# One Trainium2 kernel of a conv-attention hybrid: when the pair operands are asked for, one transfer for both copies' rows, and a table built through a skewed view

## The reference

```python
def layer0(x):                                  # 6 heads of 16 channels, 1024 tokens
    q, k, v = split(groupnorm(x) @ qkv_w + qkv_b)
    attn = (q * SCALE) @ k.T + rel_h[:, :, :, None] + rel_w[:, :, None, :]
    return x + softmax(attn) @ v @ proj_w + proj_b      # rel_w = q . rel_pos_w[w - w' + 31]
def layer1(t):
    att = where(causal, (q @ k.T) * scale, -big)        # of layernorm(t)
    return t + softmax(att) @ v @ w_proj
t = layer1(layer0(x)); out = t + experts(layernorm(t))  # top 2 of 4
```

## Time and profile before

| what | value |
|---|---|
| median of 3 runs | 2129.08 us |
| the profiled execution's own time | 2129.47 us |
| its span, first to last instruction | 2127.6 us |
| TensorE busy | 1741.9 us (82%) |
| VectorE, ScalarE, GpSimd busy | 1222.2, 1073.3, 294.8 us |
| share of the chain that ended last: PE, DVE, DMA | 53%, 20%, 12% |
| in it, waits for the transfer `qr<-negb` | 4% |
| in it, waits for `qs<-scr_rel`, for `qs<-negr` | 4%, 2% |
| mean granted TensorE clock | 0.915 of full speed |

### The profile page before, as it was taken

How to read it: one execution, slowest core, us unless ns; L and a number is a source line. 1 busy time by engine, 2 the same in 40 slices (tenths; PEclk the granted TensorE clock), 3 DMA queues, 4 the chain that set the end, 5 groups by cost and what they waited for, 6 DMA issues and landing times.

```text
span 2127.6 us, 25037 instructions
## 1 busy us (share of the span) xinstructions
PE 1741.9 (82%) x8928; PEld 694.9 (33%) x8928; DVE 1222.2 (57%) x2526; ACT 1073.3 (50%) x1375; POOL 294.8 (14%) x191
## 2 busy tenths in 40 slices
PE   1578478898799968998798987999789987989858
PEld 0122222343233433343233432334322432324333
DVE  7753657446664657636674465646576365743631
ACT  0246335574456724575355743567345753566433
POOL 5112101301023100501023010321005010200000
PEclk7589579999899989999899998999899998999979
DMA  6756371636427291555606374372816446141200
GB/s 142 140 90 127 68 166 24 103 70 160 83 54 130 52 182 26 104 84 126 114 23 116 57 175 71 62 127 55 181 24 101 80 127 107 24 68 46 39 11 8
DMA packets 73744, 188.57 MB, mean 89 GB/s; under 512 B 23188, under 2 KB 24853, under 8 KB 66964
## 3 DMA queue, kind: packets, MB, share of 16 engines
q1 hardware_dynamic: 69780, 180.18, 44.3%
q10 hardware_dynamic: 3840, 6.79, 1.3%
HBM read 115.62 MB, written 58.20 MB: 82 GB/s over the span
## 4 chain that ended last, share of the span: by engine, by line
PE 53%; DVE 20%; DMA 12%; ACT 7%; issue 4%; SPq 2%; ACTq 1%; DVEq 0%
PE psS L658 11%; DVE mx L1401 8%; PE psOM L709 6%; PE psT L832 6%; PE psT L687 5%; PE psOM L717 5%; PE psS L846 5%; DMA qr<-negb 4%; PE psT L690 4%; DMA qs<-scr_rel 4%; DVE mrow L1503 3%; DMA qs<-negr 2%; DVE qs L1530 2%; ACT probs L1087 2%; PE psT L608 2%
## 5 line engine op out<-in xcount | busy, mean ns | idle before, releaser
L1087 ACT ACTIVATE probs<-psT 128x1024 f32<-128x1024 f32 (+7 forms) x768 | 623.6, 837 | 585.4 <-PE psT L687 250.8
L1401 DVE TENSOR_REDUCE mx<-psS 128x1 f32<-128x512 f32 (+3 forms) x1152 | 681.5, 640 | 390.4 <-PE psS L658 253.4
L687 PE MATMUL psT<-qs,ks 128*128 128x512 f32 x768 | 341.1, 515 | 44.0 <-DMA qs<-negr 16.0
L658 PE MATMUL psS<-ka,qa 128*128 128x512 bf16 x768 | 305.4, 407 | 45.1 <-DVE mx L1401 26.2
L690 PE MATMUL psT<-qr,kr 97*128 97x512 bf16 (+3 forms) x576 | 194.8, 367 | 64.8 <-DMA qr<-negb 63.8
L709 PE MATMUL psOM<-probs,v 128*32 128x512 f32 x1536 | 224.8, 608 | 11.6 <-ACT probs L1087 11.6
L832 PE MATMUL psT<-xf,w1s 97*128 97x512 f32 x384 | 187.4, 622 | 1.8 <-DVE mrow L1503 1.8
L658 PEld LDWEIGHTS psS<-ka,qa 128*128 128x128 bf16 x768 | 71.8, 97 | 344.4 <-DVE mx L1401 281.3
L687 PEld LDWEIGHTS psT<-qs,ks 128*128 128x128 f32 x768 | 141.0, 197 | 125.4 <-ACT probs L1087 48.0
L846 PE MATMUL psS<-probs,w2s 128*96 128x512 f32 x384 | 180.7, 596 | 0.8 <-ACT att L1146 0.8
L1530 DVE TENSOR_TENSOR qs<-psOM,qs 32x768 fp32r<-32x768 f32 x128 | 121.8, 952 | 95.2 <-ACT qs L1121 93.4
(11 more groups left out here) (162 smaller groups left out, 1718.7 us busy)
## 6 DMA issues: line engine op xcount, KB each, us to landing
scr_rel<-qs SPq DMA_DIRECT2D x16, 1536.0 KB, 13.1
qs<-scr_rel SPq DMA_DIRECT2D x96, 256.0 KB
qs<-scr SPq DMA_DIRECT2D x144, 128.0 KB
scr<-split SPq DMA_DIRECT2D x24, 576.0 KB, 4.7
qr<-scr SPq DMA_DIRECT2D x48, 192.0 KB, 6.6
scr<-kr SPq DMA_DIRECT2D x24, 384.0 KB, 5.2
ks<-scr SPq DMA_DIRECT2D x72, 128.0 KB
qa<-scr SPq DMA_DIRECT2D x32, 192.0 KB, 5.4
```

The source lines that it names most:

```text
L658: last = mm(bank[:, 0:n], q[0:rows, h, t * P:(t + 1) * P], k[0:rows, h, kc * HALF:kc * HALF + n], start=True, stop=not diagonal)
L687: last = mm(o[:, a:b], ks[:, p % 2, hh, keys], qs[:, p % 2, kt // 2 % 2, hh, a:b], start=True, stop=True)
L1087: A(probs[:, n % 4, q0:T], psT[:, t_slot(ts, m), q0:T], ACT.Exp).then_inc(t_free, 1)
L1401: V.reduce_max(mx[layer][:, p % 2, (h % 2) * NT + t, kc:kc + 1], psS[:, s_bank(st, fill), 0:max_cols(layer, t, kc)], AX).then_inc(s_free, 1)
```

## The change

1. `attention1`: SP no longer asks for pairs 0 and 1 at its start. It waits for the spilled terms as before, gathers pair 0, waits until pair 1's row of maxima has landed, asks for layer 0's pair 0, gathers pair 1, waits for pair 2's row, asks for layer 0's pair 1, and gathers pair 2. In the prologue both loads stay where they were.
2. `attention0`: `load_pair(2)` is cut in three. The first copy is asked for where the whole was; then `gather(0, 0)`, the keys, and the second copy.
3. `attention0`: the filling of `qr`, which was the end of `spill_levels`, moves behind `gather(0, 1)`; `operands0` moves behind `gather(0, 2)`.
4. Layer 0's row of maxima goes to both copies in one transfer of 32 pieces. For that `mrow` holds the maxima twice, TensorE transposes 32 columns, and ScalarE negates 32 rows. `negmax_in` counts 16 instead of 32. The quarters stay on ScalarE's queue.
5. The table: one copy lays the row of 63 entries out 32 times with a pitch of 64, and one subtraction reads it through a view with a pitch of 63, which is skewed by one entry per row.

```diff
 def spill_levels(it, st):
     sp.dma_start(scr[:, 1, 0:2], split[:, 1, 0:2]).then_inc(spill_k, 16)
+def levels_back(it, st):
     sp.wait_ge(spill_q, upto("spill_q", it, st, 16))
     sp.wait_ge(spill_k, upto("spill_k", it, st, 16))
     fill_slots(qr, scr_d, 0, Q_SLOTS, slice(0, NH), qr_in)
...
-def load_pair(p):
+def load_copy(p, c):
     heads, slot, done = slice(2 * p, 2 * p + 2), p % 2, pair_in[p % 2]
...
+def load_pair(p):
+    load_copy(p, 0)
+    load_copy(p, 1)
+    load_keys(p)
...
 def attention1(it):
     if next_lead(it):
-        first_pairs(it - 1 if it else None, "mix")
+        spilled(it - 1 if it else None, "mix")
     for p in range(PAIRS):
         gather(it, 1, p)
+        if p + 1 < PAIRS and next_lead(it):
+            sp.wait_ge(negmax_in, upto("negmax_in", it, "attn1", 16 * (p + 1)))
+            load_pair(p)
 def attention0(it, row):
-    load_pair(2)
+    load_copy(2, 0)
     gather(it, 0, 0)
+    load_keys(2)
+    load_copy(2, 1)
     if next_layer0(it):
         spill_levels(it, "qkv0")
     gather(it, 0, 1)
     if next_layer0(it):
+        levels_back(it, "qkv0")
         sp.wait_ge(pair_in[0], upto("pair_a_in", it, "attn0", 2 * PAIR_LOADS))
         spill_wide(it, "qkv0")
+    gather(it, 0, 2)
     if next_layer0(it):
         operands0()
-    gather(it, 0, 2)
     slots1(it)
...
 def neg_max(it, layer, p):
-    A(negm[layer][:, p % 2, :], psM[0:2 * NT, 0:P], ACT.Copy, scale=-1.0).then_inc(m_free, 1)
+    A(negm[layer][:, p % 2, :], psM[0:(4 - 2 * layer) * NT, 0:P], ACT.Copy, scale=-1.0).then_inc(m_free, 1)
...
-    rows = [qr[C:C + 1, 2 * p:2 * p + 2, :]] if layer else [qs_raw[MAX_ROW:MAX_ROW + 1, p % 2, c] for c in range(2)]
-    for row in rows:
-        act.dma_start(row.rearrange("o h (t q) -> o (h t) q", q=P),
-                      negm_raw[layer][:, p % 2, :]).then_inc(negmax_in, 16)
+    if layer:
+        row = qr[C:C + 1, 2 * p:2 * p + 2, :].rearrange("o h (t q) -> o (h t) q", q=P)
+    else:
+        row = qs_raw[MAX_ROW:MAX_ROW + 1, p % 2].rearrange("o c h (t q) -> o (c h t) q", q=P)
+    act.dma_start(row, negm_raw[layer][:, p % 2, :]).then_inc(negmax_in, 16)
...
-for r in range(WS):
-    last = WIN - 1 - r
-    ins = V.tensor_scalar(relr_w[:, r, :], relf_w[:, WS - 1 - r:last + 1], relf_w[:, last:last + 1], None,
-                          ALU.subtract)
-ready(ins)
+ready(V.tensor_copy(straight, relf_w.unsqueeze(1).to_broadcast([C, WS, WIN])))
+ready(V.tensor_tensor(relr_w, skewed, skewed[:, :, WS - 1:WS].to_broadcast([C, WS, WS]), ALU.subtract))
```

More of the change, by code:

```diff
@@ L158 @@
     "rowmax": {"attn1": PAIRS - 1, "lead": 1, "attn0": PAIRS - 1},
-    "negmax_in": {"attn1": 16 * (PAIRS - 1), "lead": 32, "attn0": 32 * (PAIRS - 1), "next_mix": 16},
+    "negmax_in": {"attn1": 16 * (PAIRS - 1), "lead": 16, "attn0": 16 * (PAIRS - 1), "next_mix": 16},
     "p_used": {s: ATT_FILLS for s in _ATT},
@@ L359, in build @@
         mx = [sb(f"mx{l}", [P, 2, 2 * NT, NC]) for l in (0, 1)]
-        mrow = sb("mrow", [P, 2, 2 * NT])
-        negm = [sb("negr", [2 * NT, 2, P], F32R), sb("negb", [2 * NT, 2, P], BF16)]
+        mrow = sb("mrow", [P, 2, 2, 2 * NT])
+        negm = [sb("negr", [4 * NT, 2, P], F32R), sb("negb", [2 * NT, 2, P], BF16)]
         negm_raw = [negm[0][:, :, :].bitcast(F32), negm[1]]
@@ L375, in build @@
         relr_w = probs[0:C, 1, :].rearrange("c (a b) -> c a b", a=WS)
+        copies = probs[0:C, 2:4, :].rearrange("c s t -> c (s t)")
+        straight = copies.rearrange("c (a b) -> c a b", b=WIN + 1)[:, :, 0:WIN]
+        skewed = copies[:, WS - 1:WS - 1 + WS * WIN].rearrange("c (a b) -> c a b", b=WIN)[:, :, 0:WS]
         gs6 = sb("gs6", [C, 2, 6])
@@ L414, in build @@
         first_loads = [(cst[:, :], consts), (wqkv[0][0:C, :], w_qkv0), (wqkv[0][C:C + 1, :], b_qkv0)]
-        n_setup, n_ones = 28, 8
+        n_setup, n_ones = 29, 8
         def quarter_rows(p, c, n):
@@ L476, in operands0, with load_keys @@
                 fill_slots(ka, scr_d, 1, K_SLOTS[:4], slice(0, NH), ab_in)
-            def load_pair(p):
+            def load_copy(p, c):
                 heads, slot, done = slice(2 * p, 2 * p + 2), p % 2, pair_in[p % 2]
[L481 to L488, removed]
+                sp.dma_start(qs_raw[W_HI:W_HI + WS, slot, c], scr_rel[R_W_HI:R_W_HI + WS, heads]).then_inc(done, 16)
+                sp.dma_start(qs_raw[W_LO:W_LO + WS, slot, c], scr_rel[R_W_LO:R_W_LO + WS, heads]).then_inc(done, 16)
+                for dst, src in quarter_rows(p, c, c):
+                    sp.dma_start(dst, src).then_inc(done, 16)
+                for n, (q, _) in enumerate(S_PARTS):
+                    a = QK_ROWS + n * HD
+                    sp.dma_start(qs_raw[a:a + HD, slot, c], scr32_d[:, q, heads]).then_inc(done, 16)
+            def load_keys(p):
                 for n, (_, k) in enumerate(S_PARTS):
                     a = QK_ROWS + n * HD
-                    sp.dma_start(ks_raw[a:a + HD, slot], scr32_d[:, k, heads]).then_inc(done, 16)
+                    sp.dma_start(ks_raw[a:a + HD, p % 2], scr32_d[:, k, 2 * p:2 * p + 2]).then_inc(pair_in[p % 2], 16)
+            def load_pair(p):
+                load_copy(p, 0)
+                load_copy(p, 1)
+                load_keys(p)
             def relative(it, st):
@@ L497, in relative, with spilled @@
                 sp.dma_start(scr_rel[:, 3:NH], rel_raw[:, 3:NH]).then_inc(spill_rel, 16)
-            def first_pairs(it, st):
+            def spilled(it, st):
                 sp.wait_ge(spill_rel, upto("spill_rel", it, st, 32))
                 sp.wait_ge(rel_lead_bf, upto("rel_lead_bf", it, st, NH))
-                load_pair(0)
-                load_pair(1)
             def slots1(it):
@@ L561, in _ @@
             spill_levels(None, "p_qkv0")
+            levels_back(None, "p_qkv0")
             spill_wide(None, "p_qkv0")
@@ L564, in _ @@
             relative(None, "p_rel")
-            first_pairs(None, "p_rel")
+            spilled(None, "p_rel")
+            load_pair(0)
+            load_pair(1)
             attention0(None, 0)
@@ L667, in transpose_max @@
                 pe.wait_ge(m_free, upto("m_free", it, ms, n))
-                mm(psM[0:2 * NT, 0:P], mrow[:, p % 2, :], ident, is_transpose=True, start=True,
+                rows = (4 - 2 * layer) * NT
+                mm(psM[0:rows, 0:P], mrow[:, p % 2].rearrange("p c r -> p (c r)")[:, 0:rows], ident, is_transpose=True, start=True,
                    stop=True).then_inc(m_full, 1)
@@ L926, in first_rows @@
                 o = take_mixed(it, st, ("tmax", 0))
-                mm(o[0:2 * NT, 0:P], mrow[:, 0, :], ident, is_transpose=True, start=True, stop=True).then_inc(t_full, 1)
+                mm(o[0:2 * NT, 0:P], mrow[:, 0, 0, :], ident, is_transpose=True, start=True, stop=True).then_inc(t_full, 1)
             def group_means(it, st):
@@ L1405, in maxima @@
                         dve.wait_ge(m_full, upto("m_full", it, st, max(p - 1 - layer, 0)))
-                        V.tensor_tensor(mrow[:, p % 2, :], mx[layer][:, p % 2, :, 0], mx[layer][:, p % 2, :, 1],
-                                        ALU.max).then_inc(rowmax, 1)
+                        left, right = (mx[layer][:, p % 2, :, c].unsqueeze(1).to_broadcast([P, 2, 2 * NT]) for c in range(NC))
+                        V.tensor_tensor(mrow[:, p % 2], left, right, ALU.max).then_inc(rowmax, 1)
             def den(it, st):
@@ L1502, in first_maxima @@
                 dve.wait_ge(t_full, upto("t_full", it, st, fill + 1))
-                V.reduce_max(mrow[:, 0, n:n + 1], psT[:, t_slot(st, fill), 0:cols], AX).then_inc(t_free, 1)
+                V.reduce_max(mrow[:, 0, 0, n:n + 1], psT[:, t_slot(st, fill), 0:cols], AX).then_inc(t_free, 1)
             def expert_add(it, stage, x):
```

4 lines of the change are left out of this document (1 added, 3 removed).

## The result

The changed kernel takes 2116.14 us (median of 9 runs, 2110.16 to 2125.33) against 2129.08 us beside it: a ratio of 0.9948, 95% interval 0.9927 to 0.9969. So it is 13 us faster, 0.5% by the ratio, and not 77: more than the noise, and far under what was forecast. The profiled execution took 2110.16 us (span 2108.3; before 2127.6).

A forecast was written before the change was run, and what follows sets the result against it. TensorE, 82% busy, was taken to lose time idling, mainly on row and quarter transfers queued behind SP's loads. From 2129.47 us, -58 - 10 + 10 - 11 + 7 - 10 - 5 = -77 gave 2052 us, range 2026 to 2096.

The forecast's parts named there:

- The layer 1 row (part 1, -58): Layer 1 attention: TensorE's seven long waits for pair 1's row of maxima fall to about 0.24 us, 58 us gained.
- The lower-clock stretch behind it (-10): Behind each long wait for pair 1's row, 4.5 us at clock 0.50: 1.4 us back, seven times, 10 us gained.
- The loads' new places (+10): Loads beside layer 1's gathers: pair 2's row has 3 us in hand, layer 0's first row loses 1.5, 10 us lost.
- its sign of being wrong: Pair 2's row in layer 1 or layer 0's first row becomes a wait as long as the one that went.
- the new places collide more: Rival, chance 0.18: loads 0 and 1 beside gathers need 17 us, delaying two rows and the kt = 6 quarter; 2101 us.
- The row and quarters overtake: Rival, chance 0.14: queues served by turns, so load 1 and the filling of `qr` cost nothing; 2035 us.
- The long line: Rival, chance 0.05: a row on ScalarE's queue lands only when SP's queue is empty, later requests included; 2154 us.
- The wait isn't the loads': Rival, chance 0.03: pair 1's row is late for another reason than the loads, so 68 us stay; 2120 us.
- Part 2 (-11): Layer 0 attention: with pair 2's load cut up, 11 of 12.4 us of waits for pair 1's quarters go.
- Part 3 (+7): Layer 0 attention: the moved filling of `qr` delays pair 2's quarter for kt = 3 by 1 us, seven times, 7 us lost.
- Part 4 (-10): Layer 0's changes of pair: one row transfer lets ScalarE's last exponentials come 0.6 us earlier, 16 times, 10 us gained.
- Part 5 (-5): Prologue's table: one copy and one subtraction replace 32 instructions; gain between 0 and 13 us, 5 taken.

The follow-up runs named there:

- the held gather: The changed kernel with gather(1, 2) and what SP does behind it held until layer 0's first row has landed: 2106.73 us, ratio 0.9911 to the kernel before.

## Why the prediction was wrong

**The layer 1 row (part 1, -58): right at its place.** Pair 1's row went from 8.0 to 0.25 us, seven times. (The 16 waits before are seven long ones, eight short ones and one of 1.92 us in the first image, not two for each image as the prediction read; the sum is hardly touched.) **The lower-clock stretch behind it (-10): right at its place.** It is gone there, and came back behind the new waits (0.74 around pair 2's row, 0.50 behind layer 0's); from gather(1, 0) to pair 2's request pair 1 now takes 20.2 us (537.72 to 557.96) instead of 21.7 (556.12 to 577.80), 1.5 an image against a forecast of 1.4.

**The loads' new places (+10): this step failed.** It said that load 0 lands 3 us ahead of pair 2's row and that layer 0's row loses 1.5 us. Three things were off. The load was given 13.8 us, from a rate that the earlier trace rows shows for two loads and `xg` in one stretch; alone it takes 17.8. The row was put at the old clock's 577.80, though the step itself shortened pair 1 by 1.5 us. Together 5.5 us against 3 in hand: 2.5 late, and 2.88 measured. And layer 0's row was bounded at 4 us; it waits 7.3, because load 1 starts only 10.5 us ahead of it: at 17.8 us it ends at 590.5 by this estimate, and the row landed at 592.6, its second half beside or after the load's end. The terms that were +10 came to 7 x 2.5 + 7 x 7.3 = 69 us (2.5 is the 17.8 us of the layer 1 row that the better place took off, over 7) of waits, and new stretches of lower clock came behind them. That is about 59 of the 64 us missed, and it is what the prediction named as its sign of being wrong, a row that waits about as long as the one that went. The experiments return this by the loads' place alone: with each load before its gather the time is 2039, 13 under the forecast, and with the loads one gap earlier the same.

**The rival "the new places collide more" was the right one, under-priced.** It had the load at 17 us and both rows late, but gave them 1 and 4.5 us where 2.5 and 7.3 were measured, and nothing for the clock; its 4 us for the quarter at kt = 6 came to 1.6. It came out at 2101 where 2116 was measured, and the range ended at 2096. "The row and quarters overtake" falls: none of the row's packets moved from 583 to 586. The Trainium skill, "DMA: Bandwidth & Descriptors", section "Queues, rings and completion order", has each engine go round its queues packet by packet; the trace after, with none of the row's 48 packets moved in 3 us beside one other queue, doesn't agree with it. "The long line" falls by the held gather: 10.05 us with nothing behind it. "The wait isn't the loads'" falls with pair 1's row, which waits 0.25 us since no load stands before it.

**Part 2 (-11): right.** The 12.4 us at kt = 4 of pair 1 are gone in the kernel after, and undoing it brings 9.7 us of the quarters' waits back. **Part 3 (+7): right at its new place, wrong at its old one.** The new waits at kt = 6 of pair 2 make 9.5 us, 1.6 a time in six images. But the old place was said to cost little, as the earlier trace rows showed, and that row was read with load 2 whole. With part 2 made, the old place costs 44 us, so part 3 isn't the loss that the sum has for it. Both undone cost 3 to 6 us, where the forecast had 4 for the two together; that these agree says nothing of either part by itself.

**Part 4 (-10): right**, 11 by the time. ScalarE's request takes half the time it did in the earlier trace rows:

```profile
583.21 0.51 ACTq L1070 DMA_DIRECT2D qs<-negr  x1
```

**Part 5 (-5): a little high**, 3. VectorE is held up beside GpSimd in the kernel after, as the earlier trace rows led one to expect:

```profile
21.05 3.02 DVE L1332 TENSOR_TENSOR probs<-probs 96x1024 f32<-96x1024 f32 x1
...
25.06 2.19 DVE L1335 SCALAR_TENSOR_TENSOR lb<-lb,cst 96x63 f32<-96x63 bf16 x1
```

The second shown has 63 columns and takes 2.19 us, as long as the GpSimd instruction that starts beside it (2.12 us from 25.05); before, behind GpSimd's end, it took 0.28.

Put together for the profiled pair: +8.5 us of waits for these transfers, -10 for pair 1's clock, -11 to -16 for the joint row, -3 for the table make -15.5 to -20.5 against the -19.3 measured. The clock behind the new waits works the other way and has no price of its own here, so the list isn't closed.

## What to carry to other kernels

A transfer that is moved out of one wait needs a gap that it fits into: write down for each gap when it opens, when the next small urgent transfer is asked for, and the load's time to its last packet, not bytes over the mean rate of a busy stretch. When the moved step makes its own stage shorter, shorten the gap by it too. And a part that looks like a loss by itself should be tested with and without its neighbour: here the early filling was harmless with load 2 whole and cost 44 us with it cut up.

## What was not expected of the hardware

A load of 2.49 MB begins at 0.18 MB/us and goes on at 0.12 (0.61 MB in 5 us) with the engines still 96% busy; its last 0.17 MB fill 22% of the engines' time in the stretch that they end in. A row of 32 pieces asked for under a load moved in two halves of 24 packets, some 3 us apart, and landed in 9.4 us; one asked for in the quiet landed in 2.2 us (the loads one gap earlier), and one of 16 pieces in 1.7.
